# The end of a quantised FFN on one core: transfer order, joined maxima, and three pieces in halves

## What is computed

```python
def _act_fake_quant(x, clip_factor):
    scale = sigmoid(clip_factor) * max(abs(x)) / 127
    return clip(round(x / scale), -128, 127) * scale
def _weight_fake_quant(w):
    scale = max(abs(w), axis=1, keepdims=True) / 127
    return clip(round(w / scale), -128, 127) * scale
def ffn(x, clip_x, clip_down, w_gate, w_up, w_down):   # x: 8 x 1024 x 512, hidden size 1408
    xq   = _act_fake_quant(x, clip_x)
    gate = einsum('bsh,ih->bsi', xq, _weight_fake_quant(w_gate))
    up   = einsum('bsh,ih->bsi', xq, _weight_fake_quant(w_up))
    h    = _act_fake_quant(silu(gate) * up, clip_down)
    return einsum('bsi,hi->bsh', h, _weight_fake_quant(w_down))
x = x + ffn(layernorm(x), ...)
```

## Time and profile before

| what | us |
|---|---|
| median of three runs | 1272.61 |
| the profiled execution, device time | 1272.64 |
| its span in the trace | 1270.8 |
| PE busy in it | 1249.2 (98%) |
| DVE busy | 1104.5 (87%) |
| ACT busy | 796.9 (63%) |
| POOL busy | 288.7 (23%) |
| last product of the up stage ends, about | 1106.8 |
| products of the down stage, first start and last end | 1112.7, 1266.7 |

### The profile page before, as it was taken

How to read it: one execution, slowest core, us unless ns; L and a number is a source line. 1 busy time by engine, 2 the same in 40 slices (tenths; PEclk the granted TensorE clock), 3 DMA queues, 4 the chain that set the end, 5 groups by cost and what they waited for, 6 DMA issues and landing times.

```text
span 1270.8 us, 20478 instructions
## 1 busy us (share of the span) xinstructions
PE 1249.2 (98%) x7576; PEld 586.4 (46%) x7620; DVE 1104.5 (87%) x2127; ACT 796.9 (63%) x1209; POOL 288.7 (23%) x227
## 2 busy tenths in 40 slices
PE   6999999999999999999999999999999999999998
PEld 4644444444444444444444445444444444444443
DVE  7776888988988898898889859899999999799998
ACT  7578686567658756756775672333433333399994
POOL 2104331342144134214403420000000000013223
PEclk9999999999999999999999999999999999999999
DMA  8275257246255353363562391386656652489997
GB/s 306 75 242 182 34 158 220 79 133 202 66 173 166 105 191 105 116 216 84 154 220 92 100 267 69 99 278 265 235 204 265 225 189 83 149 291 424 422 423 301
DMA packets 171108, 241.74 MB, mean 190 GB/s; under 512 B 122096, under 2 KB 141312, under 8 KB 154880
## 3 DMA queue, kind: packets, MB, share of 16 engines
q1 hardware_dynamic: 171008, 240.43, 56.2%
HBM read 120.86 MB, written 90.57 MB: 166 GB/s over the span
## 4 chain that ended last, share of the span: by engine, by line
PE 73%; ACT 9%; DVE 8%; DMA 6%; issue 2%; SPq 2%; POOL 1%; DVEq 0%; ACTq 0%; POOLq 0%
PE bank L1690 10%; PE bank L1694 10%; PE po L77 9%; PE po L79 8%; PE po L78 8%; PE ring L79 7%; PE ring L78 7%; PE ring L77 7%; ACT hb L1527 5%; DMA xa<-x_rows_d 2%; DMA out_dram<-xa 2%; PE ring L1086 2%; PE bank L1731 1%; PE ring L1113 1%; DMA x<-in_x_dram 1%
## 5 line engine op out<-in xcount | busy, mean ns | idle before, releaser
L1511 ACT ACTIVATE sg<-bank,gate_scale 128x512 f32<-128x512 f32 x176 | 120.8, 687 | 184.0 <-PE bank L1690 174.0
L77 PE MATMUL ring<-yT,M 128*128 128x512 f16 x512 | 194.1, 379 | 0.0
L78 PE MATMUL ring<-yT,M 128*128 128x512 f16 x512 | 194.0, 379 | 0.0
L79 PE MATMUL ring<-yT,M 128*128 128x512 f16 x512 | 194.0, 379 | 0.0
L77 PE MATMUL po<-VW,p 128*128 128x512 f16 x480 | 182.2, 380 | 0.0
L78 PE MATMUL po<-VW,p 128*128 128x512 f16 x480 | 181.9, 379 | 0.0
L79 PE MATMUL po<-VW,p 128*128 128x512 f16 x480 | 181.9, 379 | 0.0
L1690 PE MATMUL bank<-xqT,w 128*128 128x512 bf16 x682 | 176.8, 379 | 1.5 <-DMA xqT<-xq 0.7
L1694 PE MATMUL bank<-xqT,w 128*128 128x512 bf16 x682 | 176.7, 379 | 0.7
L481 ACT ACTIVATE p<-E 128x512 f16<-128x512 f32 x120 | 74.6, 624 | 132.7 <-DVE E L678 132.6
L1731 PE MATMUL bank<-w 128*128 128x512 bf16 x690 | 151.8, 379 | 3.1 <-DVE w L1646 2.3
(11 more groups left out here) (266 smaller groups left out, 1945.9 us busy)
## 6 DMA issues: line engine op xcount, KB each, us to landing
hidden<-hb SPq DMA_DIRECT2D x11, 2816.0 KB, 8.9
xa<-x_rows_d SPq DMA_DIRECT2D x28, 1024.0 KB, 6.0
hb<-hidden SPq DMA_DIRECT2D x22, 1024.0 KB, 14.8
x<-in_x_dram SPq DMA_DIRECT2D x16, 1024.0 KB, 5.3
value_fold<-E SPq DMA_DIRECT2D x64, 256.0 KB, 2.5
VW<-value_fold SPq DMA_DIRECT2D x16, 1024.0 KB, 6.1
x_rows_d<-x SPq DMA_DIRECT2D x16, 1024.0 KB, 4.2
out_dram<-xa SPq DMA_DIRECT2D x11, 1024.0 KB, 10.3
```

What stands on the lines that cost most here:

```text
L77: nc.tensor.matmul(out, a_hi, b_hi, start=first, stop=False)
L78: nc.tensor.matmul(out, a_hi, b_lo, start=False, stop=False)
L79: return nc.tensor.matmul(out, a_lo, b_hi, start=False, stop=last)
L1511: nc.scalar.activation(sg[:, n % 4], pg[n % 4][:], ACT.Silu, scale=gate_scale[:, n % FT:n % FT + 1]).then_inc(silus, 1)
```

## The change

Six things, all in `ffn`:

1. SP: in its round 8 only load_h(14) is left. Round 9 begins with load_h(15), then load_r(11) and store(8), and goes on as before with store(9) and load_r(12). Before, the order was load_h(14), store(8), load_r(11), load_h(15), store(9), load_r(12).
2. In the last group of the up stage each tile's maximum is scaled and joined as soon as it is there (`join`), with `reach` of a tile right behind its `hidden`; the multiplication and the reduction of the 15 groups before are made beside the group's first tile. The factor with the clip is divided out ahead of time (`clip_scale`, beside the second tile).
3. The last up product is made in halves of 256 tokens in two banks, and `hidden`, `reach` and `join` of it too.
4. Behind POOL's maximum, DVE makes one reciprocal and `hscale`; the factor `one[6]` is made after that and not ahead of it.
5. The first tile of block 0 is scaled by ACT and rounded by DVE in halves of 256 tokens; PE waits for the first half at t = 0 and for the second at t = 2.
6. The last output tile (block 15, t = 3) is made in two halves of 256 columns, in `pg[3]` and `pu[3]`, with `scale_down`, add and store in halves too.

```diff
@@ SP
-        sp.wait_ge(ups, NG * FT)
+        sp.wait_ge(ups, NG * FT + 1)
...
         for q in range(NG):
             if q + 6 < NG:
                 load_h(q + 6)
+            if q + 7 == NG - 1:
+                continue
+            if q + 6 == NG - 1:
+                load_r(q + 2)
+                store(q - 1)
             slot = r_slot(q)
             if q < NG - 1:
-                sp.wait_ge(added, 2 * q + 2)
-                sp.wait_ge(added_too, 2 * q + 2)
...
+                store(q)
             else:
-                for t in range(TT):
+                for t in range(TT - 1):
...
+                for k, half in enumerate(COL_HALVES):
+                    sp.wait_ge(added_too, 2 * q + TT - 2 + k)
+                    sp.dma_start(og[taken_as(q)][:, TT - 1, half], xa[slot][:, TT - 1, half]).then_inc(out_stored[slot], 16)
@@ ACT
             for m in range(FT):
-                nc.scalar.activation(hb[:, slot, m], hb[:, slot, m], ACT.Identity, scale=hscale[:, m:m + 1], bias=magic[:, 0:1]).then_inc(h_scaled, 1)
+                for part in token_halves if q == 0 and m == 0 else (slice(0, GT),):
+                    nc.scalar.activation(hb[:, slot, m, part], hb[:, slot, m, part], ACT.Identity, scale=hscale[:, m:m + 1], bias=magic[:, 0:1]).then_inc(h_scaled, 1)
@@ DVE, end of the up stage
-        dve.wait_ge(hmaxs, NG)
-        do_(nc.vector.tensor_tensor(hmax[:], hmax[:], hscale[:], ALU.mult))
-        nc.vector.tensor_reduce(one[:, 1:2], hmax[:], AX.X, ALU.max).then_inc(range_in, 1)
+        def join(col, i, to):
+            dve.wait_ge(reaches, FT * last + col + 1)
+            dve.wait_ge(last_max, col + 1)
+            return nc.vector.scalar_tensor_tensor(to, hmax_g[:, col:col + 1], hscale[:, i:i + 1], one[:, 8:9], ALU.mult, ALU.max)
+        for i in range(FT - 1):
+            hidden(last, i)
+            if i == 0:
+                do_(nc.vector.tensor_tensor(hmax[:], hmax[:], hscale[:], ALU.mult))
+                nc.vector.tensor_reduce(one[:, 8:9], hmax[:], AX.X, ALU.max).then_inc(last_max, 1)
+            if i == 1:
+                do_(nc.vector.reciprocal(one[:, 9:10], keep.clips[:, 1:2]))
+                do_(nc.vector.tensor_scalar(clip_scale[:], hscale[:], one[:, 9:10], None, ALU.mult))
+            reach(last, i)
+            join(i, i, one[:, 8:9]).then_inc(last_max, 1)
+        halves = (slice(0, GT // 2), slice(GT // 2, GT))
+        last_hidden(halves[0], 0)
+        last_reach(halves[0], 0)
+        join(FT - 1, FT - 1, one[:, 8:9]).then_inc(last_max, 1)
+        last_hidden(halves[1], 1)
+        last_reach(halves[1], 1)
+        join(FT, FT - 1, one[:, 1:2]).then_inc(range_in, 1)
         dve.wait_ge(range_all, 2)
+        do_(nc.vector.reciprocal(one[:, 7:8], one[:, 5:6]))
+        nc.vector.tensor_scalar(hscale[:], clip_scale[:], one[:, 7:8], None, ALU.mult).then_inc(down_scales, 1)
         do_(nc.vector.tensor_tensor(one[:, 6:7], one[:, 5:6], keep.clips[:, 1:2], ALU.mult))
-        do_(nc.vector.reciprocal(one[:, 7:8], one[:, 6:7]))
-        nc.vector.tensor_scalar(hscale[:], hscale[:], one[:, 7:8], None, ALU.mult).then_inc(down_scales, 1)
@@ DVE, down stage
-        for n in range(FT):
+        for k, part in enumerate(token_halves):
+            dve.wait_ge(h_scaled, k + 1)
+            nc.vector.tensor_scalar(hq[:, 0, 0, part], hb[:, h_slot(0), 0, part], MAGIC, QMAX, ALU.subtract, ALU.min).then_inc(h_step, 1)
+            dve.wait_ge(h_step, k + 1)
+            nc.vector.tensor_scalar(hq[:, 0, 0, part], hq[:, 0, 0, part], -QMAX - 1.0, QMAX, ALU.max, ALU.min).then_inc(h_rounded, 1)
+        for n in range(1, FT):
             round_h(0, n)
...
+        for k, half in enumerate(COL_HALVES):
+            dve.wait_ge(downs, 4 * last + TT + k)
+            nc.vector.tensor_tensor(sg[:, tile, half], (pg[tile], pu[tile])[k][:, half], down[:, half], ALU.mult).then_inc(down_taken, 1)
+            dve.wait_ge(down_taken, 4 * last + TT + k)
+            nc.vector.tensor_tensor(xa[slot][:, tile, half], xa[slot][:, tile, half], sg[:, tile, half], ALU.add).then_inc(added_too, 1)
@@ PE
-            for c in range(DC):
-                ins = nc.tensor.matmul(pu[n % 4][:], wu[:, c, at], xqT[:, g % 2, c], start=(c == 0), stop=(c == DC - 1))
-            ins.then_inc(ups, 1)
+            for k, half in enumerate(halves if n == NG * FT - 1 else (slice(0, GT),)):
+                if k == 1:
+                    pe.wait_ge(hs, n - 2)
+                for c in range(DC):
+                    ins = nc.tensor.matmul(pu[(n + k) % 4][:, half], wu[:, c, at], xqT[:, g % 2, c, half], start=(c == 0), stop=(c == DC - 1))
+                ins.then_inc(ups, 1)
...
                 for t in range(TT):
+                    if q == 0 and m == 0 and t < 3:
+                        pe.wait_ge(h_rounded, 1 + t // 2)
...
+                if q == NG - 1 and t == TT - 1:
+                    pe.wait_ge(down_taken, 4 * q)
+                    for to, half in zip((pg[t], pu[t]), COL_HALVES):
+                        for m in range(FT):
+                            ins = nc.tensor.matmul(to[:, half], hq[:, q % 2, m, t * P:(t + 1) * P], wd[:, m, half], start=(m == 0), stop=(m == FT - 1))
+                        ins.then_inc(downs, 1)
+                    continue
```

More of the change, by code:

```diff
@@ L1296, in ffn @@
     hmax = sb("hmax", [P, FT], fp32)
-    hmax_g = sb("hmax_g", [P, FT], fp32)
+    hmax_g = sb("hmax_g", [P, FT + 1], fp32)
+    clip_scale = sb("clip_scale", [P, FT], fp32)
     down = sb("down", [P, D], fp32)
@@ L1335, in ffn @@
     scales_ready, ones_set = sem("scales_ready"), sem("ones_set")
+    last_max = sem("last_max")
     h_loaded = [sem(f"h_loaded{k}") for k in range(5)]
@@ L1352, in ffn @@
     BY_BLOCK = 12
-    parts_before = lambda q: sum(len(parts(k)) for k in range(q))
+    parts_before = lambda q: sum(len(parts(k)) for k in range(q)) + 1
+    token_halves = (slice(0, GT // 2), slice(GT // 2, GT))
     sums_of = lambda q: pu if q % 2 == 0 else pg
@@ L1461, in on_sync, with store @@
         load_h(5)
+        def store(q):
+            slot = r_slot(q)
+            sp.wait_ge(added, 2 * q + 2)
+            sp.wait_ge(added_too, 2 * q + 2)
+            if slot == ODD:
+                sp.dma_start(og[taken_as(q)][:, 0:2], spare_pair).then_inc(out_stored[slot], 16)
+                for t in (2, 3):
+                    sp.dma_start(og[taken_as(q)][:, t], r_tile(slot, t)).then_inc(out_stored[slot], 16)
+            else:
+                sp.dma_start(og[taken_as(q)], xa[slot]).then_inc(out_stored[slot], 16)
         for q in range(NG):
@@ L1487, in on_sync @@
             whole = 3 if k == ODD else sum(1 for q in range(NG - 1) if r_slot(q) == k)
-            sp.wait_ge(out_stored[k], 16 * whole + (16 * TT if k == r_slot(NG - 1) else 0))
+            sp.wait_ge(out_stored[k], 16 * whole + (16 * (TT + 1) if k == r_slot(NG - 1) else 0))
     def on_gpsimd(pool):
@@ L1614, in on_vector @@
                 wait(dve, h_stored[HOME[g]], 16 * stores_of(HOME[g], g))
+            if g == NG - 1:
+                break
             for i in range(FT):
@@ L1622, in on_vector, with last_hidden @@
             dve.wait_ge(reaches, FT * (g + 1))
-            nc.vector.tensor_tensor(hmax[:], hmax[:], hmax_g[:], ALU.max).then_inc(hmaxs, 1)
-        dve.wait_ge(hmaxs, NG)
-        do_(nc.vector.tensor_tensor(hmax[:], hmax[:], hscale[:], ALU.mult))
-        nc.vector.tensor_reduce(one[:, 1:2], hmax[:], AX.X, ALU.max).then_inc(range_in, 1)
+            nc.vector.tensor_tensor(hmax[:], hmax[:], hmax_g[:, 0:FT], ALU.max).then_inc(hmaxs, 1)
+        def last_hidden(part, k):
+            n, i = FT * NG - 1, FT - 1
+            dve.wait_ge(silus, n + 1)
+            dve.wait_ge(ups, n + 1 + k)
+            nc.vector.tensor_tensor(hb[:, HOME[last], i, part], pu[(n + k) % 4][:, part], sg[:, n % 4, part], ALU.mult).then_inc(hs, 1)
@@ new lines, in last_reach @@
+        def last_reach(part, k):
+            dve.wait_ge(hs, FT * NG + k)
+            nc.vector.tensor_reduce(hmax_g[:, FT - 1 + k:FT + k], hb[:, HOME[last], FT - 1, part], AX.X, ALU.max, apply_absolute_value=True).then_inc(reaches, 1)
+        def join(col, i, to):
+            dve.wait_ge(reaches, FT * last + col + 1)
+            dve.wait_ge(last_max, col + 1)
+            return nc.vector.scalar_tensor_tensor(to, hmax_g[:, col:col + 1], hscale[:, i:i + 1], one[:, 8:9], ALU.mult, ALU.max)
@@ new lines, in on_vector @@
+        last = NG - 1
+        dve.wait_ge(hmaxs, last)
+        for i in range(FT - 1):
[8 more added lines that the diff above has]
+            join(i, i, one[:, 8:9]).then_inc(last_max, 1)
@@ L1676, in on_vector @@
                     round_h(q + 1, n)
-            for t in range(TT):
+            for t in range(TT if q < NG - 1 else TT - 1):
                 scale_down(q, t)
@@ L1680, in on_vector @@
                     add_rows(q, t)
+        last, tile, slot = NG - 1, TT - 1, r_slot(NG - 1)
+        for k, half in enumerate(COL_HALVES):
```

(6 more changed lines are left out.)

11 lines of the change are left out of this document (3 added, 8 removed).

## The result

| | kernel before | changed kernel |
|---|---|---|
| median, us | 1272.33 (20 runs) | 1273.43 (20 runs) |
| lowest to highest | 1270.96 to 1273.39 | 1272.16 to 1276.1 |
| profiled execution, span | 1272.64, 1270.8 | 1274.05, 1271.9 |

The ratio to the kernel before is 1.0013 with a 95% interval of [1.0007, 1.0019]: 0.9 to 2.4 us slower, within the 0.2% that I called no change, where the forecast of +1.7 us (1.0013) had put it.

A forecast was written before the change was run, and what follows sets the result against it. PE was taken as the slowest in the down stage, losing time only where it stands. Opening -0.5, transfers +2.3 and tail -0.1 gave +1.7 on 1272.64, so 1274.3 us; range 1271.3 to 1276.0.

The forecast's parts named there:

- the load is not late where it matters: Rival on row load 11: it lands as before and block 14's stall stays, 1272.0 us; chance 0.15.
- both rivals in which DVE itself would be the limit: Apparently block 14's second-stall rival (DVE needs over 9.5 us, chance 0.23) and last_third_late's (DVE, not the transfer, late).
- the second stall stays: Rival at part 1 of block 14: the 1.1 us stall taken off remains, 1275.4 us; chance 0.23.
- the margin of 0.4: Part 1 of block 14: DVE rounds it at 1250.2, PE wants it at 1250.6, so 0.4 us is left.
- DVE was to wait 4.2 us: DVE's round 12: it stands from 1231.4 to 1235.6, waiting for the rows of block 11.
- PE was to stand 3.4: Block 13, m = 4: part 1 is rounded at 1241.1, PE wants it at 1237.7, so PE stands 3.4 us.
- from bytes and rate: Row load 11: 2.88 MB put ahead and one store taken away at 423 GB/s, landing 4.3 us later at 1235.6.
- one stall over 3 us: Sign in the profile after: PE has one stall over 3 us in block 13 and none in block 14.
- the tail's change of at most 0.3: Sign at the end: from last product to last landing nothing changes by more than 0.3 us.
- The rule that I weighed: DMA queue: ring order gives +2.3 us; completion not first in, first out could let row load 11 overtake, giving 0.
- The opening: Parts 2 to 5, between the stages: ACT 0.7 us and PE 1.05 sooner, block 2 0.5 sooner; bounds 0.2 to 1.05.
- The tail: Part 6, last output tile in halves: gain 0.1 us, bounds 0 to 0.5.

The follow-up runs named there:

- order_undone: The changed kernel without part 1, so the transfers go in the order of before; 1271.34 us, ratio 0.9995 to the kernel before.
- order_alone: The kernel before with part 1 of the change alone; 1274.96 us, ratio 1.0021 to the kernel before.
- last_block_late: order_undone with the whole last h block (2816 KB) issued behind row load 12; 1270.72 us, ratio 0.9986 to the kernel before.
- filled_stall: The changed kernel with 10 unused PE products where PE stands before part 1 of block 13; 1273.29 us, ratio 1.0011 to the kernel before.
- filled_again: filled_stall run once more, beside changed_again on one chip; 1273.25 us, ratio 1.0014 to the kernel before.
- changed_again: The changed kernel run once more, unaltered, as partner of filled_again on one chip; 1275.1 us, ratio 1.0023 to the kernel before.
- last_third_late: order_undone with only the last third (768 KB) of the last h block issued behind row load 12; 1271.04 us, ratio 0.9991 to the kernel before.
- two_thirds_ahead: The changed kernel with row load 11 between the second and last third of the last h block; 1272.67 us, one execution.

## Why the prediction was right

**The transfer was the right mechanism.** I put the sum at -0.5 + 2.3 - 0.1 and the measured ratio is the forecast's. The chain I named is in the trace step by step: row load 11 behind 2.88 MB, POOL's longer idle, DVE's new wait in its round 12, PE's stall before part 1 of block 13, no stall in block 14. The runs order_undone and order_alone tell it from the rival that the load is not late where it matters, and last_block_late from both rivals in which DVE itself would be the limit. The rival that the second stall stays fell too: PE has no stall behind 1239.12, on the margin of 0.4. The half clock had put PE 1.7 us later there, which helps; but filled_stall and filled_again have the full clock and no stall in block 14 either.

**It was right in part by errors that cancel.** DVE was to wait 4.2 us and waited 2.98 (3.83 in changed_again); PE was to stand 3.4 and stood 2.12 (2.97). The slack between the two was right: 0.8 in the sum, 0.86 in the traces. The step that was mis-sized is the landing time "from bytes and rate": not 4.3 us later but 2.5 (1231.2 before, 1233.7 now; the load of order_undone landed at 1231.0), and 3.7 in changed_again. Why it is less than the bytes say isn't shown. Two things are: the same load in the same queue lands 1.2 us apart from one execution of the changed kernel to another; and in the trace of before, on which I built, the next transfer, the first third of h block 15 with 1024 KB, landed 0.9 us behind it (issued 1208.16, 23.9 us to landing), where its bytes take 2.5. So the load of before may have been late for its place, and I had read its time as the rule.

Against this stands a cost that no step had: the half clock behind the stall, 1.7 us. 2.12 + 1.7 = 3.8, for my 3.4. Taken off are the stall of before in block 14, 1.1, and 0.2 at the part behind it (from block 2 to the last product before took 134.47 us, 1.31 more than last_block_late): +2.5 to 2.6 where I had 2.3. That the median came out near the forecast is luck beyond this: half of the executions have a lowered mean clock and half don't, with medians of 1274.7 and 1272.9 us. The forecast of 1274.3 lies between the two, and had no step that tells them apart. Two of the signs that I gave failed: "one stall over 3 us", and the tail's change of at most 0.3.

The rule that I weighed, that completion is not first in, first out for one issuing engine (the Trainium skill, DMA: Bandwidth & Descriptors, "Queues, rings and completion order"), did not decide here: the row load landed behind what was put ahead of it each time, and DVE's wait for it was longer by 0.95 with the last 768 KB ahead. The first half of that rule, ring order, is the one to reckon with.

**The opening** was 0.35 for my 0.5, inside its bounds; ACT 0.64 sooner for 0.7, PE's start 1.09 for 1.05, and block 2 took the rest back as described. But the inner terms were wrong: I gave the halves of the up product a gain of their own, and they cost 0.35; the joins alone are worth 1.0.

**The tail** was 0.83 for 0.1, outside its bounds of 0 to 0.5. Two terms failed. One is the last store: the forecast has its 0.3 us of bytes and then leaves it out of the 0.1 without a reason; it measured 0.31. The other is "DVE is busy to 1266.43 with the add of t = 2 (1.29 us, beside POOL)". That was true in the profile of before, where PE's last product ends 8.5 us behind the start of the `scale_down` of block 14, and it is as true in order_undone and last_third_late (8.6 in both), where the halves save 0.45. In the changed kernel the distance is 10.4 us, in last_block_late 9.8: DVE is further ahead of PE, the add runs alone in 0.69, and DVE is there when the first half is. I had carried a row over into a schedule that the change itself had shifted.

## What to carry to other kernels

When one DMA queue is full, its order is a schedule: ask of each transfer when it is wanted, put the one with the least slack first, and look at who waits for the one that is pushed back; here the last input of ACT had some 6 us to spare (in the kernel before its last third landed at about 1238.1, and ACT began that block at 1244.7) and the rows of DVE had none. A stall of PE can cost more than its length, since the clock behind it may be halved. So two short stalls may be cheaper than one long one: two_thirds_ahead, with 1.17 and 0.54 us, kept the full clock, but it is one execution. A time of a trace is one draw: before building on when a transfer lands, read it in several executions. Halving a piece to overlap two engines pays only if the second engine is free when the first half comes; otherwise it adds its fixed costs, as it did between the stages, and at the tail it paid 0.8 us where DVE was free and 0.45 where it wasn't. The best kernel of the set is not the change as it was made: with the joins, the tail in halves and the last h block issued last it ran at 1269.79 us, 0.9984 [0.9975, 0.9992] of before.

## What the runs showed of the hardware that was not expected

- PE's granted clock went from 2.4 to 1.2 GHz for some 3.4 us behind idle times of 2.12, 2.16 and 2.97 us, ahead of which PE had run without a break, at 1.7 us each time; it stayed at full behind idle times of 1.09 and 1.17 us, and when 10 unused products filled all but 0.45 us of the idle time. At the start of the program it fell behind 2.19, 2.22 and 2.29 us and in none of the eleven profiles with 0.61 to 1.78 us there.
- PE's stall was DVE's wait less 0.86 or 0.87 us in four traces with waits from 2.03 to 3.83 us: a transfer's lateness went to PE one for one once the slack was used up.
- A row load of 1024 KB with the same transfers ahead of it let DVE go at 1233.75, 1234.92 and 1234.44 in three executions (changed kernel, changed_again, filled_again), 1.2 us apart, where PE's first down product differs by 0.3 at most. Its issue differs too, 1208.65, 1209.36 and 1209.02: 0.7 of the 1.2.
- A multiplication or a reduction of DVE on 256 columns of f32 (`hidden`, `reach`) takes 0.42 us to the 0.69 of one on 512: 61% of the time for half the work.
- An add of DVE on 512 columns with both inputs in SBUF takes 0.69 us alone and 1.27 to 1.29 beside POOL's adds.
